# Routing work one attention slot sooner, a new closing order, and fewer barriers in a four-phase kernel on one core

## What is computed

```python
# L0 attention: 16 heads of 16; heads are a plain reshape of (t, dm), rotary, softmax
xq = (x @ wq.T + bq).reshape(b, h, t, d)            # likewise xk, xv
p = softmax(einsum('bhqd,bhkd->bhqk', xq, xk) / sqrt(d))
o = einsum('bhqk,bhkd->bhqd', p, xv).transpose(0, 2, 1, 3).reshape(b, t, dm) @ wo.T + bo
# x = x + o, layer norm, then L0 ffn: 8 experts, 2 chosen
probs = softmax(x @ router_weight); top 2 of 8
y1, y2 = split(x @ w1[e]); g = silu(y1) * y2; out = sum_e (g @ w2[e]) * probs[e]
# L1 attention: a Mamba block (scan over 512 steps, 512 inner channels, 16 states), with its residual
# L1 ffn: 8 linear experts, 2 chosen, weights from a clipped softmax
```

## Time and profile before

| what | us |
|---|---|
| median of 3 runs (2392.2 to 2396.88) | 2396.49 |
| the profiled execution's own time | 2396.72 |
| its span in the profile | 2394.9 |
| attention phase, from the start to the last engine at its end barrier | 767.8 |
| first instruction of the expert phase | 769.3 |
| first instruction of the Mamba phase | 1053.6 |
| first instruction of the last phase | 2097.8 |

### The profile page before, as it was taken

How to read it: one execution, slowest core, us unless ns; L and a number is a source line. 1 busy time by engine, 2 the same in 40 slices (tenths; PEclk the granted TensorE clock), 3 DMA queues, 4 the chain that set the end, 5 groups by cost and what they waited for, 6 DMA issues and landing times. The chain is left out here.

```text
span 2394.9 us, 33044 instructions
## 1 busy us (share of the span) xinstructions
PE 1975.1 (82%) x10006; PEld 1160.5 (48%) x10006; DVE 1727.0 (72%) x2430; ACT 1208.0 (50%) x2459; POOL 1452.0 (61%) x1149
## 2 busy tenths in 40 slices
PE   2599999999972999946889898989898987659998
PEld 1234444444432999933334343434343433347776
DVE  4577777777734655521999999999999999746554
ACT  1066656666551433315675757575757565222322
POOL 7344435433334344421999999998989999634444
PEclk9899999999875999967999898989898999868999
DMA  3444435433243344421230303030303040011100
GB/s 86 99 101 103 103 81 120 110 86 101 60 136 126 61 76 77 74 57 55 104 133 27 133 27 135 25 136 24 136 24 139 12 142 9 7 57 36 35 27 26
DMA packets 230818, 185.86 MB, mean 78 GB/s; under 512 B 148329, under 2 KB 201201, under 8 KB 230658
## 3 DMA queue, kind: packets, MB, share of 16 engines
q1 hardware_dynamic: 215778, 162.87, 24.1%
q0 software_dynamic: 13296, 17.77, 4.3%
q10 hardware_dynamic: 1584, 3.24, 0.4%
HBM read 134.33 MB, written 49.49 MB: 77 GB/s over the span
## 5 line engine op out<-in xcount | busy, mean ns | idle before, releaser
L1694 POOL TENSOR_TENSOR mb_dbu<-mb_dtu,mb_bbc 128x1024 f32<-128x1024 f32 x256 | 601.6, 2362 | 72.8 <-DVE mb_hp L1836 47.4
L459 ACT ACTIVATE ex_plain<-at_t_ps 128x512 f32<-128x512 f32 x512 | 294.8, 595 | 216.1 <-PE at_t_ps L845 210.7
L1899 PE MATMUL mb_y_ps<-mb_hc,mb_ident 128*128 128x512 f32 x640 | 329.7, 641 | 76.8 <-DVE mb_hc L1844 76.8
L599 DVE TENSOR_REDUCE at_mx<-at_s_ps 128x2 f32<-128x1024 f32 x256 | 311.0, 1220 | 95.7 <-PE at_s_ps L854 95.5
L1838 DVE TENSOR_TENSOR_SCAN mb_da_ps<-mb_da_ps,mb_dbu 128x1024 f32<-128x1024 f32 x160 | 365.2, 2283 | 17.2 <-ACT mb_da_ps L1747 17.2
L845 PE MATMUL at_t_ps<-ex_w 64*128 64x512 f32 x512 | 214.0, 503 | 44.0 <-ACT ex_plain L459 38.1
L1899 PEld LDWEIGHTS mb_y_ps<-mb_hc,mb_ident 128*128 128x128 f32 x640 | 124.6, 204 | 245.3 <-issue 125.1
L1700 POOL TENSOR_TENSOR mb_hp<-mb_hp,mb_cbc 128x1024 f32<-128x1024 f32 x96 | 226.7, 2361 | 0.0
L1836 DVE TENSOR_TENSOR_SCAN mb_hp<-mb_da_ps,mb_dbu 128x1024 f32<-128x1024 f32 x96 | 218.8, 2279 | 0.0
L1133 POOL DMA_INDIRECT x<-m_o,m_xs x71 | 113.9, 1604 | 172.1 <-DMA x<-m_o,m_xs 99.4
L1844 DVE TENSOR_TENSOR mb_hc<-mb_da_ps,mb_cbc 128x1024 f32<-128x1024 f32 x160 | 195.9, 1225 | 19.4 <-PE mb_y_ps L1899 2.1
(11 more groups left out here) (313 smaller groups left out, 4196.3 us busy)
## 6 DMA issues: line engine op xcount, KB each, us to landing
mb_bbc<-mb_scr SPq DMA_DIRECT2D x64, 512.0 KB, 6.1
mb_cbc<-mb_scr SPq DMA_DIRECT2D x64, 512.0 KB, 4.8
ex_w<-at_scr SPq DMA_DIRECT2D x384, 64.0 KB, 2.3
m_xs<-rt_rows SPq DMA_DIRECT2D x71, 129.0 KB, 2.2
at_scr<-at_qk_hi SPq DMA_DIRECT2D x32, 256.0 KB
at_scr<-at_qk_lo SPq DMA_DIRECT2D x32, 256.0 KB
at_xin<-in_x SPq DMA_DIRECT2D x32, 128.0 KB, 2.2
ex_plain<-in_x SPq DMA_DIRECT2D x8, 512.0 KB
```

What stands on the lines that cost most here:

```text
L459: act.activation(probs[:, c, h, :], t_ps[:, k % 2, :], ACT.Exp, scale=SCALE).then_inc(exp_done, 1)
L599: dve.tensor_reduce(out, s_ps[:, m % 2, :, :], AX.X, ALU.max).then_inc(max_done, 1)
L1694: pool.tensor_tensor(dbu[:, q % 3, :, :], dtu_2, bbc[:, 2 * p:2 * p + 2, :], ALU.mult).then_inc(S["dbu_ready"], 1)
L1899: last = pe.matmul(y_ps[:, v % 2, :], ident[:, :], src[:, j, :], start=(q == tile_first[v] and j == 0), stop=(q == tile_last[v] and j == 1))
```

## The change

`project_out` moves from slot u + 5 to slot u + 4, and every routing lag falls by one: the load of the batch's input (3 to 2), the bias (5 to 4), variances, `log_var` and the store (9 to 8), `newton` and `normalise` (10 to 9), `rows_T` (11 to 10), `logits` and `shares` (12 to 11), `choose`, `ranks`, `copy_rows` (13 to 12), `places` (14 to 13), `scatter` (14 and 15 to 13 and 14). In slot 32 no output product is made. The closing sequence is written anew: batch 6's routing stands ahead of the output products 28 and 29, its ranks between 29 and 30, and batch 7's steps behind those. `EARLY` becomes 5: experts 1 to 4 get their lower parts on DVE behind the table, experts 2 to 4 their upper parts at ACT's end. The barriers and the clearing between phases go, but for one clearing (now of both phases' semaphores) and one barrier behind the expert phase.

```diff
-    EARLY = 3
+    EARLY = 5
@@ sync
-                    if (n := batch(t, 9)) is not None:
+                    if (n := batch(t, 8)) is not None:
                         store(n)
-                    if (n := batch(t, 3)) is not None:
+                    if (n := batch(t, 2)) is not None:
...
-                store(NB - 2)
@@ gpsimd
-                    if (n := batch(t, 5)) is not None:
+                    if (n := batch(t, 4)) is not None:
                         add_bias(n)
...
-                        if (n := batch(t, 14 + c)) is not None:
+                        if (n := batch(t, 13 + c)) is not None:
                             scatter(n, c)
-                    if t == 28:
+                    if t == 27:
                         experts.lower_parts(pool, 0)
-                add_bias(NB - 1)
@@ scalar, after the loop
-                copy_rows(n - 1, 0)
-                copy_rows(n - 1, 2)
+                for a in range(4):
+                    normalise(n, a)
                 act.wait_ge(pv_done, 4 * NT)
                 experts.load(act, A, 5)
+                exp_logits(n)
+                copy_rows(n, 0)
+                copy_rows(n, 2)
                 experts.upper_parts(act, 1)
...
-                experts.upper_parts(act, 2)
+                for k in range(2, Experts.EARLY):
+                    experts.upper_parts(act, k)
@@ vector, after the loop
                 n = NB - 2
-                choose(n - 1, 0)
-                choose(n - 1, 1)
-                add_tile(4 * n + 3, f_ps)
-                tile_stats(4 * n + 3)
-                variances(n)
-                rank_rows(n - 1, t_ps[:, 0, :])
                 places(n - 1)
                 newton(n)
+                take_rows(n, 0, t_ps[:, 1, :])
+                take_rows(n, 1, o_ps[:, :])
+                differences(n, f_ps)
+                shares(n)
+                choose(n, 0)
+                choose(n, 1)
                 for a in range(4):
                     add_tile(4 * n + 4 + a, s_ps[:, a // 2, a % 2, :])
                     tile_stats(4 * n + 4 + a)
                     if a == 1:
-                        take_rows(n, 0, t_ps[:, 1, :])
-                        take_rows(n, 1, o_ps[:, :])
+                        rank_rows(n, t_ps[:, 0, :])
+                        places(n)
                 variances(n + 1)
-                experts.lower_parts(dve, 1)
-                differences(n, f_ps)
                 newton(n + 1)
-                shares(n)
-                choose(n, 0)
-                choose(n, 1)
...
-                experts.lower_parts(dve, 2)
+                for k in range(1, Experts.EARLY):
+                    experts.lower_parts(dve, k)
@@ tensor
-                        if k == 15 and (u := tile(t - 5)) is not None:
+                        if k == 15 and t < NT and (u := tile(t - 4)) is not None:
                             project_out(u, f_ps)
...
-                ranks(n - 1, t_ps[:, 0, :])
+                rows_T(n, 0, t_ps[:, 1, :])
+                pe.wait_ge(oc_ready, NT)
+                rows_T(n, 1, o_ps[:, :])
+                pe.wait_ge(R["r_run"], n)
+                for a in range(4):
+                    logits(n, a, f_ps)
                 for a in range(4):
                     project_out(4 * n + 4 + a, s_ps[:, a // 2, a % 2, :])
                     if a == 1:
-                        rows_T(n, 0, t_ps[:, 1, :])
...
+                        ranks(n, t_ps[:, 0, :])
@@ four_phases
+    used = []
     for phase, ends in phases:
-        used = []
...
         if phase is moe_swiglu_phase:
             route_ctx.close()
-            used += kept
-        if phase is not moe_linear_phase:
-            nc.all_engine_barrier()
-            nc.clear_and_free_semaphores(used)
+            nc.clear_and_free_semaphores(kept + used)
             nc.all_engine_barrier()
```

More of the change, by code:

```diff
@@ L518, in _ @@
                             act.activation(rs[:, u % 4, 1:2], rs[:, u % 4, 0:1], ACT.Exp, scale=-0.5).then_inc(rsq_done, 1)
[L519 removed]
+                        if t == 27 and k == 1:
                             experts.upper_parts(act, 0)
[L521 removed]
+                        if k == 13 and (n := batch(t, 8)) is not None:
                             log_var(n)
[L523 removed]
+                        if k == 14 and (n := batch(t, 8)) is not None:
                             inverse_root(n)
[L525 removed]
+                        if k in (4, 7, 10, 13) and (n := batch(t, 9)) is not None:
                             normalise(n, (k - 4) // 3)
[L527 removed]
+                        if k == 7 and (n := batch(t, 11)) is not None:
                             exp_logits(n)
[L529 removed]
+                        if k in (6, 10) and (n := batch(t, 12)) is not None:
                             copy_rows(n, 2 * (k == 10))
                 n = NB - 2
[L532 to L533 removed]
+                for a in range(4):
+                    normalise(n, a)
                 act.wait_ge(pv_done, 4 * NT)
                 experts.load(act, A, 5)
+                exp_logits(n)
+                copy_rows(n, 0)
+                copy_rows(n, 2)
                 experts.upper_parts(act, 1)
[L537 to L541, removed]
                 log_var(n + 1)
                 inverse_root(n + 1)
[L544 removed]
                 for a in range(4):
@@ L549, in _ @@
                 experts.load(act, A, 6)
-                copy_rows(n, 2)
                 exp_logits(n + 1)
@@ L694, in _ @@
                     ahead = tile(t + 2)
-                    if (p := tile(t - 6)) is not None:
+                    if (p := tile(t - 5)) is not None:
                         add_tile(p, f_ps)
@@ L699, in _ @@
                         dve.wait_ge(R["r_const"], 16 * N_RCONST)
-                    if (n := batch(t, 10)) is not None:
+                    if (n := batch(t, 9)) is not None:
                         newton(n)
-                    if (n := batch(t, 13)) is not None:
+                    if (n := batch(t, 12)) is not None:
                         choose(n, 0)
@@ L708, in _ @@
                                           ALU.subtract, ALU.mult).then_inc(xn_ready, 1)
+                    if (n := batch(t, 10)) is not None:
+                        take_rows(n, 0, f_ps)
                     if (n := batch(t, 11)) is not None:
-                        take_rows(n, 0, f_ps)
-                    if (n := batch(t, 12)) is not None:
                         differences(n, f_ps)
                     max_pair(ahead, 1)
-                    if (p := tile(t - 6)) is not None:
+                    if (p := tile(t - 5)) is not None:
                         tile_stats(p)
@@ L720, in _ @@
                     max_pair(ahead, 2)
-                    if (n := batch(t, 9)) is not None:
+                    if (n := batch(t, 8)) is not None:
                         variances(n)
+                    if (n := batch(t, 12)) is not None:
+                        choose(n, 1)
                     if (n := batch(t, 13)) is not None:
-                        choose(n, 1)
-                    if (n := batch(t, 14)) is not None:
                         places(n)
@@ L754, in _ @@
                     max_pair(ahead, 6)
+                    if (n := batch(t, 10)) is not None:
+                        take_rows(n, 1, f_ps)
+                    if (n := batch(t, 12)) is not None:
+                        rank_rows(n, f_ps)
                     if (n := batch(t, 11)) is not None:
[L756 to L759, removed]
                         shares(n)
@@ L941, in _ @@
                             values(t, (k - 6) // 4)
-                        if k == 13 and (n := batch(t, 11)) is not None:
+                        if k == 13 and (n := batch(t, 10)) is not None:
                             for free in f_free:
@@ L946, in _ @@
                             f_free = ((R["r_T"], 2 * n + 2),)
-                        if k == 13 and (n := batch(t, 13)) is not None:
+                        if k == 13 and (n := batch(t, 12)) is not None:
                             for free in f_free:
@@ L951, in _ @@
                             f_free = ((R["r_run"], n + 1),)
-                        if k == 2 and (n := batch(t, 11)) is not None:
+                        if k == 2 and (n := batch(t, 10)) is not None:
                             for free in f_free:
@@ L959, in _ @@
                             f_free = ((R["r_T"], 2 * n + 1),)
-                        if k < 4 and (n := batch(t, 12)) is not None:
+                        if k < 4 and (n := batch(t, 11)) is not None:
                             for free in f_free:
```

5 lines of the change are left out of this document (1 added, 4 removed).

## The result

| | before | changed |
|---|---|---|
| median of 14 runs each | 2394.34 | 2403.87 |
| lowest and highest | 2385.13, 2402.41 | 2396.50, 2405.23 |
| the profiled execution: own time, span | 2396.72, 2394.9 | 2403.99, 2402.2 |

The ratio is 1.0036, with an interval of 1.0020 to 1.0052: slower, by some 8.6 us, with a lower end at the bound of what can be told from no change. A second measurement of the same two kernels gave 1.0005 only; it stands last among the experiments. The profiled executions differ by 7.3 us. By phase boundaries, that is: attention block end +11.7, the way from there into the experts -1.3, experts -0.9, the way into Mamba +0.3, Mamba -1.9, the way into the last phase -1.0, last phase +0.4.

The account below looks back on a forecast made before the run. PE was taken to pace the attention loop, then a serial chain and POOL's scatter queue; block end +7.6, barriers -1.2 and -1.0, experts -2.2 sum to +3.2: 2399.9, as a median 2399.7, range 2390.5 to 2407.0.

Parts of the forecast that it names:

- the mean is 1.65, for three 5.0: Block tail: three last scatters beside DVE's subtractions are each held 1.65 on average, 5.0 us in all.
- the second rival: Block tail: subtractions hold the scatters to the end of the last pair, +4.9 more, 2404.6, slower; chance 0.19.
- the block end of +7.6: Attention block's end: last scatter ends at 768.3, drain follows for 7.15, block ends at 775.4 instead of 767.8.
- The first rival: Block tail: subtractions don't hold the scatters, the sum loses 5.0, 2394.7, no change; chance 0.15.
- The steps of batch 6: Closing order: DVE held by POOL's bias until about 714.4, normalised by 717.3, scatters from 731.8, 5.0 sooner.
- The sequence of batch 7: Closing order: its steps now follow batch 6's chain; places at 751.7 against 745.56, 6.2 later, 4.7 of it the loop.
- L: Attention loop: how much later it ends, 4.7 us, from one more product (2.0) and batch 5's logits (2.7).
- The 2.7 of the logits: Loop's end: batch 5's logits move to slot 31, two pieces of 1.06 plus 0.6 waiting for DVE's sum.
- The rivals of the clock and of overlap: Loop clock stays high, 2390.7 (0.12); or sequenced closing steps overlap or late logits use idle time, DVE unheld, 2394.5 (0.11).
- the third rival: Slots 30 and 31: PE's clock stays high, its busy time shrinking by up to 9.8 us; 2390.7 at 9; chance 0.12.
- Experts 3 and 4: Expert phase: splitting these two ahead saves 1.1 us each in their slots, -2.2, bounds 0 and -3.
- this passes through: Expert phase: its end follows its last tiles, so the 2.2 us saved at the slots shortens the phase.

Follow-up runs that it names:

- the gaps version: Changed kernel with ACT's upper parts sooner, DVE's lower parts of experts 1 to 3 in its waits for PE, expert 4's behind the scatters; 2398.66, ratio 1.0000.
- the run with the unread products: Kernel before with PE products nobody reads added: four of 128x256 in slot 4, eight small ones in slot 31; median 2400.34, ratio 1.0017.
- the order alone: Changed kernel with EARLY = 3 and the old barriers, so only the new timetable and closing order; median 2401.36, ratio 1.0030.

## Why the prediction was right or wrong

**The sum.** Predicted +3.2, measured +7.3 between the two profiled executions. The block's end is 4.1 later than predicted, by one term; what the other terms miss cancels (experts +1.3, Mamba -1.9, the rest +0.6). The mechanism, a serial chain and then a hold by the subtractions, was right, and the price of the hold was not. The range 2390.5 to 2407.0 holds both measured medians of the changed kernel; that the same two kernels differ by 0.36% in one measurement and 0.05% in another is nothing that the prediction had.

**The hold was sized wrong.** The step was "the mean is 1.65, for three 5.0". It was 9.5 (10.48 instead of 0.97). The three scatters were not each held a little: the first was held until DVE's last subtraction, the others came after it, at 772.17, where the second rival put them at 773.2. So the second rival is what happened, and the block end of +7.6 was +11.7. The step took a mean over two rows, and the earlier trace rows held the answer apart: the 1.92 beside a pair was let through between its two instructions, the 3.33 was not. In the runs a scatter was held by two, four, six and eight subtractions for 2.4, 4.7, 7.2 and 9.5 us, and it ended 0.85 to 0.87 after the last of them. Early release was seen at 1.92, in the gaps version at 2.02, and also within a longer row, the table's three two-input operations without a pause between them (kernel before):

```profile
747.38 0.73 DVE L811 TENSOR_TENSOR at_xin<-at_slot_no,at_ends 1x568 f32<-1x568 f32 x1
747.51 1.46 POOL L390 DMA_INDIRECT rt_rows<-at_pay,at_pos  x1 [0.28 <-POOL at_pay L384]
748.04 0.73 DVE L812 TENSOR_TENSOR at_wraw<-at_slot_no,at_starts 1x568 f32<-1x568 f32 x1
```

That scatter ends 0.86 after the first of them. What goes with the difference, in the closing sequence of all twelve traces, is the start. Each of the seven scatters that were held for a whole row of subtractions started no later than 0.06 us after the first of them; those that started 0.10 us or more after the start of a two-input operation waited for that one alone. Why that is so was not tested.

**The first rival fell.** Without the second SBUF input there is no hold (0.96 to 0.98 beside the eight operations), with it there is one in each run that has scatters and such subtractions side by side.

**Right in mechanism and size.** The steps of batch 6: held by POOL's bias (2.25), normalised at 717.15 (717.3), scatters from 731.52 (731.8). The sequence of batch 7: places at 751.33 (751.7). The 3.58 of the 16 logits, cited from the earlier trace rows, is no row there, but it is in the trace. That these absolute times came so close is in part luck, since the loop's end alone moves by 17 us from one execution to another. Into the experts -1.3 (-1.2), into the last phase -1.0 (-1.0). Behind the experts +0.3 was measured where 0 was taken, within its bounds.

**The loop.** L was 4.7, measured 5.4 at the last exponential. That looks right and is only half shown. 2.1 us of it are slot 4, repeated by the run with the unread products. The 2.7 of the logits could not be seen in that run. The rest is mixed with a change of clock (below). One slot of the changed kernel alone, the counterpart of the one of 20.09 us in the kernel before, is 4.1 longer by its clock, and others are shorter (the columns are those of the earlier trace rows):

```profile
372.93:397.12 24.19, 23.85 (x183) 11.81 (x175) 14.15 (x22) 11.49 (x24) 11.35 (x18) 0.79 0.43 106
```

Over five executions of old timetables the last exponential ended at 690 to 701, over six with the new one at 691 to 708, means 6 apart. The two ranges overlap nearly wholly, so that the agreement of 5.4 with 4.7 is in part luck.

**The rivals of the clock and of overlap.** Slots 30 and 31 had 0.75 and 0.73, not full clock, so the third rival's gain did not come. Nothing overlapped that was put in sequence. From the last exponential's end to the places of batch 7 are 48.6 us, before 48.3, where the prediction had 1.5 more; over all executions they are 48.6 to 50.7 with the new order and 47.8 to 49.0 with the old one, means 1.6 apart.

**Experts 3 and 4.** Their slots gave 2.6 (2.2 predicted), but the whole phase only 0.9. The difference isn't at the slots: the first rows landed 4.4 us after the phase's first instruction instead of 3.7, and POOL's last additions follow each other in 4.5 to 4.9 instead of 4.4. The other traces show that this was one execution. With three experts early the phase takes 282.8 to 283.3 us in four executions; with five early 282.4, 281.3, 280.5, 279.8, 279.7 and 279.1 in six. Their means are 2.6 apart, so that the 2.2 and "this passes through" were right, and the changed kernel's first execution had the longest of the six.

**Mamba.** -1.9 between the two executions, where nothing was changed and the prediction had 0. It is not this one execution alone: the changed kernel's second one has a phase of 1040.6 us, where the first had 1041.2 and the kernel before 1043.1. But it does not go with the change either: the old order with its subtractions moved has 1040.8 and 1040.7, the order alone 1041.8, the gaps version 1043.9, and the other three versions of the old timetable 1043.5 to 1044.1. The cause stays open.

## What to carry to other kernels

Before work is put on an idle VectorE, look at what GpSimd does beside it: an elementwise operation with two SBUF inputs held an indirect DMA for the whole unbroken row of them, 10.48 us instead of 0.97, and it did so here at the one point where POOL's queue ended the block. Give such a row another place: behind the last transfer, under the drain, or in pairs in VectorE's waits, where no scatter took more than 2.02. An operand in PSUM took the hold away too. When two rows of a trace disagree about a hold, do not take their mean: look at what started first, and where the transfer starts with the row or ahead of it, count the whole unbroken row.

## What the runs showed of the hardware

**The same slot at two clocks.** The changes of a few us were measured against a loop that by itself varies by more. These windows cover two equally built slots of the attention loop, in the kernel before:

```profile
292.61:310.55 17.94, 16.89 (x166) 7.84 (x158) 13.70 (x20) 11.72 (x25) 7.12 (x14) 1.00 0.38 84
310.55:334.74 24.19, 23.86 (x183) 11.79 (x175) 14.14 (x22) 11.49 (x24) 7.08 (x14) 0.79 0.41 84
389.23:409.32 20.09, 19.67 (x186) 10.34 (x178) 14.52 (x22) 11.51 (x24) 11.24 (x18) 1.00 0.52 127
```

and the same two in the version with only the barriers changed, whose loop is identical:

```profile
308.90:328.95 20.05, 19.62 (x187) 10.33 (x179) 13.95 (x22) 11.52 (x24) 7.13 (x13) 1.00 0.50 101
383.44:407.64 24.20, 23.87 (x186) 11.72 (x179) 14.15 (x22) 11.51 (x24) 11.39 (x18) 0.79 0.43 105
```

Once the first is 24.2 us and the second 20.1, once the other way round: 4.1 us for one slot. They are among the loop's densest: PE is busy for 19.62 of the 20.05 us. Within the slow one, windows of 3 us in the kernel before:

```profile
313.00:316.00 3.00, 3.00 (x17) 1.45 (x18) 1.91 (x3) 1.33 (x3) 1.89 (x6) 1.00 0.62 93
316.00:319.00 3.00, 2.85 (x15) 1.75 (x13) 0.86 (x3) 0.93 (x2) 0.00 (x0) 1.00 0.92 232
319.00:322.00 3.00, 3.00 (x15) 1.00 (x14) 1.45 (x2) 0.86 (x2) 0.00 (x0) 0.60 0.99 194
322.00:325.00 3.00, 3.00 (x12) 2.30 (x11) 0.14 (x1) 1.08 (x2) 0.00 (x0) 0.50 0.28 78
```

The level fell from 2.4 to 1.2 GHz (0.50) after PE had been busy for 5.85 of 6 us, and the next slot had 1.00 throughout. The changed kernel had three such slots of 24.2 us in its first profile and two, with one of 21.4, in the second. A few of them more or less in an execution are enough for the spread of its runs, 2389 to 2405, and for the short profile of the order alone. What decides it in one execution stays open.

**GpSimd's drain** after the last indirect DMA took 5.3 us in every version, whether DVE was subtracting beside it or not. From the last scatter's end to the block's end lie 7.2 to 7.4 us, but for the version with all subtractions behind the scatters, where DVE ends the block 11.5 after it.
